# The experts' routing-weight multiply, moved from GpSimd to VectorE, in a fused two-layer attention and experts kernel

## What is computed

```python
def expert_body(y, args):
    w13_e, w2_e, c_e = args
    h = _silu_and_mul(xt @ w13_e.T)
    return (y + c_e[:, None] * (h @ w2_e.T), None)
y, _ = lax.scan(expert_body, jnp.zeros_like(xt), (w13, w2, comb.T))
y = y + _silu_and_mul(xt @ w13_s.T) @ w2_s.T
```

## Time and profile before

| | us |
|---|---|
| median of 3 runs (lowest to highest) | 1751.99 (1751.29 to 1755.93) |
| the profiled execution | 1752.64 |
| its span | 1750.8 |
| VectorE busy | 1214.8 (69% of the span) |
| TensorE busy (matmul) | 967.0 (55%) |
| ScalarE busy | 556.0 (32%) |
| GpSimd busy | 118.9 (7%) |

### The profile page before, as it was taken

The page is one execution under the profiler, slowest core; times in us unless marked ns, Lnnn a source line. Parts: engine busy times, 40 slices in busy tenths (PEclk is TensorE's granted clock), DMA queues, the critical chain, the costliest instruction groups (busy, mean ns, idle before and its releaser), DMA issues. The chain is left out here.

```text
span 1750.8 us, 29056 instructions
## 1 busy us (share of the span) xinstructions
PE 967.0 (55%) x10272; PEld 600.1 (34%) x10272; DVE 1214.8 (69%) x3031; ACT 556.0 (32%) x1210; POOL 118.9 (7%) x168
## 2 busy tenths in 40 slices
PE   4555564656455675476536556556635667354454
PEld 2443452434133252244324235234413335131112
DVE  4566763667699874476689886467779996534995
ACT  2332222535232320354433221244524321044220
POOL 0000000111001000020101000002100000020000
PEclk8575675788567786687767777678858787686586
DMA  3000000200113100110012200020022210021220
GB/s 115 1 8 8 8 2 13 50 7 1 57 49 73 31 2 7 38 26 8 5 65 70 71 1 2 13 49 8 1 57 61 69 23 2 14 48 35 83 76 7
DMA packets 48741, 55.34 MB, mean 32 GB/s; under 512 B 21200, under 2 KB 27344, under 8 KB 48400
## 3 DMA queue, kind: packets, MB, share of 16 engines
q1 hardware_dynamic: 48592, 53.42, 12.1%
HBM read 49.73 MB, written 3.67 MB: 31 GB/s over the span
## 5 line engine op out<-in xcount | busy, mean ns | idle before, releaser
L687 PE MATMUL bank<-tparts,onehot 128*128 128x64 bf16 x3840 | 164.6, 210 | 74.3 <-DVE onehot L1406 74.1
L687 PEld LDWEIGHTS bank<-tparts,onehot 128*128 128x128 bf16 x3840 | 154.6, 110 | 98.6 <-issue 55.1
L1636 DVE TENSOR_TENSOR_SCAN SG<-big 128x512 f32<-128x512 f32 x128 | 150.6, 1218 | 6.9 <-DVE GT L1422 2.1
L1406 DVE TENSOR_SCALAR onehot<-ib,CO 128x512 bf16<-128x512 f16 x320 | 106.6, 395 | 54.3 <-ACT ib L995 46.0
L995 ACT ACTIVATE ib<-bank 128x512 f16<-128x512 f32 x128 | 75.9, 596 | 180.5 <-PE bank L672 179.5
L833 PE MATMUL bank<-CV,CO 128*128 128x512 f32 x128 | 92.2, 860 | 43.3 <-DVE CV L1646 43.3
L833 PE MATMUL bank<-XP,CO 128*128 128x512 f32 x128 | 80.6, 762 | 62.3 <-DVE XP L1646 62.1
L1119 ACT ACTIVATE big<-DEL,Aneg 128x512 f32<-128x512 f32 x128 | 84.7, 717 | 63.8 <-DVE SG L1636 52.8
L960 ACT ACTIVATE relu_s<-bank,nml 128x192 f32<-128x192 f32 (+1 forms) x128 | 53.0, 426 | 162.5 <-DVE nml L1367 162.5
L1190 POOL TENSOR_TENSOR g_s<-G,trig 128x128 f32<-128x128 f32 x64 | 40.1, 626 | 934.1 <-ACT G L1008 934.1
L510 PE MATMUL bank<-CO,relu_s 128*128 128x128 f32 (+2 forms) x256 | 47.0, 346 | 68.4 <-ACT relu_s L960 68.4
(11 more groups left out here) (306 smaller groups left out, 2163.6 us busy)
## 6 DMA issues: line engine op xcount, KB each, us to landing
BC<-bc_rows SPq DMA_DIRECT2D x128, 256.0 KB, 4.4
big<-comb_rows SPq DMA_DIRECT2D x8, 1024.0 KB, 10.0
rows_bounce<-RO SPq DMA_DIRECT2D x256, 8.5 KB
W<-w SPq DMA_DIRECT2D x1, 2818.0 KB, 14.8
RB<-rows_bounce SPq DMA_DIRECT2D x16, 136.0 KB, 2.1
X<-x SPq DMA_DIRECT2D x4, 256.0 KB, 2.9
out<-CV SPq DMA_DIRECT2D x4, 256.0 KB, 2.5
big<-w SPq DMA_DIRECT2D x1, 576.0 KB, 7.5
```

Source lines behind the costliest of these rows:

```text
L687: m = mm(bank[2 + c % 2][:, (4 * (r % 2) + q) * 64:(4 * (r % 2) + q + 1) * 64], onehot[:, r % 2, kt, q * P:(q + 1) * P], tparts[:, kt, par ...
L1406: m = TS(onehot[:, r % 2, kt, :], ib[:, r % 2, :], co("pos")[:, kt:kt + 1], None, ALU.is_equal)
L1636: m = dve.tensor_tensor_scan(hs[:, j, :], dA[:, n % 2, j, :], dBu[:, n % 2, j, :], 0.0, ALU.mult, ALU.add)
```

## The change

The multiply by the routing weights is taken out of GpSimd's program and put into VectorE's, right behind the product with the up projection. The waits for `y_part` (the buffer `HT` is free) and `cb_sb` (the routing weights have landed) go with it.

```diff
             def rest(b, alone=False):
 
                 pool.wait_ge(rest_done.sem, rest_done.at(b, 0))
-                for _ in range(ROUTE_PHASES + 1):
-                    yield
-                for p in range(8):
-                    pool.wait_ge(hu_ok.sem, hu_ok.at(b, p + 1))
-                    if p >= 1 + alone:
-                        pool.wait_ge(y_part.sem, y_part.at(b, p - alone))
-                    pool.wait_ge(cb_sb.sem, cb_sb.at(b, 2))
-                    pool.tensor_tensor(HT_turn[turn_of(alone, p)], SG_turn[turn_of(alone, p)][:, 1, :], CB[:, p, :], ALU.mult).then_inc(ht_ok.sem, ht_ok.up())
-                    yield
-                    yield
-                for _ in range(EXPERT_PHASES - 17 + NORM_PHASES + SCAN_IN_PHASES + DS + SCAN_OUT_PHASES + NORM_PHASES + TOP1_PHASES):
+                for _ in range(ROUTE_PHASES + EXPERT_PHASES + NORM_PHASES + SCAN_IN_PHASES + DS + SCAN_OUT_PHASES + NORM_PHASES + TOP1_PHASES):
                     yield
...
                     TT(dst, SGp[0:rows, 1, :], bank[k0 + 1][0:rows, :], ALU.mult).then_inc(hu_ok.sem, hu_ok.up())
                     dve.wait_ge(hu_ok.sem, hu_ok.now(b))
+                    if p < 8:
+                        if p >= 1 + alone:
+                            dve.wait_ge(y_part.sem, y_part.at(b, p - alone))
+                        dve.wait_ge(cb_sb.sem, cb_sb.at(b, 2))
+                        TT(HT_turn[turn_of(alone, p)], SGp[:, 1, :], CB[:, p, :], ALU.mult).then_inc(ht_ok.sem, ht_ok.up())
                     yield
```

## The result

| | before | after |
|---|---|---|
| median (lowest to highest), 22 runs each | 1751.14 (1744.23 to 1755.96) | 1756.93 (1746.65 to 1761.86) |
| ratio, 95% interval | | 1.003 (1.0019 to 1.0042) |
| the profiled execution, its span | 1752.64, 1750.8 | 1757.68, 1755.9 |

The changed kernel comes out 0.3% slower where 0.17% faster was forecast. Two repeats, beside other runs of the kernel before, gave less: 1.0012 (0.9987 to 1.0036) and 0.9998 (0.9986 to 1.001), 12 runs each. Over all 46 runs of the changed kernel the mean is 1754.7 us, over all 171 of the kernel before 1751.0. So the loss is some 4 us, 0.2%, and one set of runs can miss it by over 0.2%.

What follows compares the result with a forecast made beforehand. No engine was full, VectorE fullest; nothing in the woven rows waited for the multiply's result, only the last stage's chain did. Woven rows -0.5 and last stage -2.4 gave -2.9 us: 1749.1 us as median, range 1743.5 to 1755.

Steps and rivals of the forecast that it cites:

- The price of the multiply: One multiply on VectorE, start to start: 0.83 us, bounds 0.69 (waits free) and 0.93; 24 in the woven rows, 19.9 us.
- p = 0: First pair, woven rows: the multiply fits into VectorE's 2.52 us idle before ScalarE's logs, 0.7 us to spare; cost 0.
- p = 1 to p = 4: Woven-row pairs: faster comparisons, no sine wait and faster copies against 0.83 us each; net 0, -0.3, -1.05, +0.36 us.
- the walk: Pair-by-pair costs in woven row 1, including +0.83 us at the sixth pair and 0 at the next two; sum -0.16 us.
- The sum of the woven rows' pairs: Three woven rows at -0.16 us each, -0.5 us: 19.9 us of new VectorE work comes out at about nothing.
- rows 2 and 3 of the program repeat its pattern: Assumption that the costs found in row 1 hold in the other two woven rows, so -0.16 us each.
- The refunds: VectorE time regained per woven row: 1.28 us in comparisons at p = 2, 1.88 for sines, 0.47 in copies.
- The rival that the refunds fail: Gather rounds wait for ScalarE's copy of `G`, so p = 2 to p = 5 cost 0.83 each: +7.6 us, 1759.6; chance 0.07.
- The port that both engines share: VectorE and GpSimd lock each other out: comparison pairs 1.6 to 1.9 us beside GpSimd's multiply, 0.62 without; sine products could collide.
- The last stage: Row 3's `rest` alone, multiply in the serial chain: -0.57 us at p = 0, -0.61 at p = 2, 4, 6; sum -2.4.
- an us is left for TensorE's clock: Last allowance in the range's upper end, beyond 1753.9 us: 1 us for the clock falling otherwise in single stretches, giving 1755.
- three signs that the prediction names of being wrong: VectorE waits for `y_part`; the pairs' stage grows over a us per row; or the last stage keeps its length.

## Why the prediction was wrong, step by step

- **The price of the multiply** was taken as 0.83 us (0.69 to 0.93) and measured 0.72 at p = 1, 3, 4 and 5 and 0.62 at p = 2 in the two rows of the loop, and 0.61 throughout in the row that is written out, where a dependent instruction starts 0.72 us after its product instead of 0.83 to 0.94. Right in kind, a little too dear.
- **p = 0** cost nothing in the woven rows, as said: the only wait of VectorE for the spread weights is the 7.3 us of the last stage.
- **p = 1 to p = 4.** The comparisons fell to 0.61 us, the 1.98 us for the sines went, the `PBD` copies lost 0.47. Where the forecast had a doubt, that later rounds may be less well fed, it was justified: up to the next subtraction p = 2 gained 0.94 us, and 0.82 of it came back in the round behind, by the new wait of 0.76 for the sines.
- **Term by term** the walk is off by more than its sum. Change of the time from one product with the up projection to the next (us, means of three profiles each):

| behind p | forecast | rows 0 and 1, each | row 2 |
|---|---|---|---|
| 0 | 0 | 0.01 | -0.09 |
| 1 | 0 | +0.26 | +0.21 |
| 2 | -0.3 | -0.21 | +0.12 |
| 3 | -1.05 | -1.48 | -1.54 |
| 4 | +0.36 | +0.51 | +1.72 |
| 5 | +0.83 | +0.58 | +0.55 |
| 6 | 0 | -1.05 | -0.67 |
| 7 | 0 | +0.58 | -0.02 |
| ahead of p = 0 and behind p = 8 | not treated | +0.48 | 0.00 |
| sum | -0.16 | -0.3 | +0.3 |

- **The sum of the woven rows' pairs** was -0.5 us and came out at -0.3, means of three profiles each. That the two agree so closely is luck: single profiles of the changed kernel lie between 322.1 and 326.9 us, p = 3, 4, 6 and 7 were mis-sized and cancelled, and "rows 2 and 3 of the program repeat its pattern" fails at p = 4 of the row that is written out. The refunds were put at 3.5 us a row (1.13, 1.88 and 0.47) and the multiplies at 3.3; the kernel with no multiply puts them at 1.6 and, against the 324.4 us with one, 1.5. The claim that 16 to 20 us of new work on the fullest engine come to about nothing in these stages stands. The rival that the refunds fail wanted 10.0 us more in these stages and falls. It would have named about the right sign for the wrong reason.
- **The port that both engines share.** The exclusive lock that the Trainium skill describes (page "SBUF — State Buffer", section "Who interferes with whom") fits the comparisons: 1.6 to 1.9 us beside GpSimd's multiply, 0.61 without it. Its other half, that the new multiply would collide with the sine products, no run here shows: not one of the 128 sine products lies in time over a multiply. That an instruction of VectorE with two inputs in SBUF is held up beside GpSimd does show, in the combining product of 1.14 us instead of 0.29.
- **The last stage** was put at -2.4 us and gave -4.9 (means), -4.5 in the first pair of profiles. The mechanism held: in the first pair, in the forecast's terms, -0.82 at p = 0 (forecast -0.57), then -0.68, -1.59 and -0.68 for three periods (-0.61 each), and -0.78 behind them (nothing). The term left out is TensorE's clock, at the full level for 27 us, in which TensorE waits 1.46 to 1.99 us for `HT` at a time instead of 2.21 to 2.66. That the shorter gaps kept the clock up is argued, not tested alone; but the last pairs took 56.0 to 56.4 us in all twelve profiles with VectorE's multiply there and 59.0 to 62.8 in all eight with GpSimd's.
- **The step that failed** is the last one of the range: "an us is left for TensorE's clock". The sum priced only the stages whose code changes and let all others keep their length. They took 9.2 us more, 7.0 of it in the norm and scan-out stages. Without that the result would have been -0.3 - 4.9 = -5.2 us, some 1747, inside the range; with it, it is +4.0. None of the three signs that the prediction names of being wrong could have told: they look at the stages whose code changes, VectorE never waits for `y_part`, the pairs stay within 1 us a row by the means, and the last stage is shorter.
- **Busy times** were forecast at about 1231 and 78 and came out at 1226.6 and 78.6.

Within the stages compared above, the clock is the cause of the length: the same matmuls take longer at the low level, and VectorE's longer waits for their results make up 3.1 of 3.1 us and 3.4 of 3.7. What stays open is why the change lets the clock be low there more often, and what the pairs have to look like for the short form. The +9.2 us rest on three profiles each, which lie from 1058.9 to 1063.0 and from 1065.8 to 1073.4 us (the changed kernel's third comes from another chip), and the scans' 1.6 us of them were not traced to a cause. They could not be switched on and off by one edit; the nearest to it is the doubled multiply, three profiles of which have the short forms in rows 0 and 1, with norm stages of 75.3 to 76.5 us.

## What to carry to other kernels

Where TensorE is little more than half busy and its clock changes level many times, an edit that moves instructions by less than a us is worth what the stages downstream make of it. Cut the profile into stages and compare those whose code is the same: what they gain or lose is the edit's too, and a forecast from the touched stages alone needs, by the spread seen here, some +-10 us in 1750 for it. Take the part of a change that pays by itself: here the last row on VectorE, which won 0.3%, and with GpSimd's multiply one phase later 0.6%. And repeat a verdict of 0.3% in another set of runs: of three for the same kernel one said 1.003 and one 0.9998.

## What was not expected of the hardware

- Lengths of the same stage recur to some 0.1 us between kernels and executions, as if there were a few forms of it: in rows 0 and 1 most are 75.0 to 75.5, 77.2 to 77.4 or 79.0 to 79.1 us for the norm, and 35.0 to 35.1, 35.9 to 36.1 or 38.0 us for the scan-out. The Trainium skill (page "TensorE: Matmul & The Clock Gate", section "Part 1: The HAM clock gate (the "warmup" mystery)") says that the same kernel sees a different number of slow matmuls from run to run and puts the penalty of the slow start at under 1% of a typical kernel. The traces agree with the first: row 0's norm stage of the kernel before was granted 0.59 of the clock in one execution and 0.67 in the other, and the stretch to the first route, the same code in all, took 297.6 to 306.7 us in twenty profiles. The second speaks of the start, and here the level changes all through the kernel; the 9.2 us are 0.5% of it and were enough to turn the sign.
- On VectorE the multiply never got slower in company. The changed kernel's view of the tile `HT` (shortest, median and longest in ns, first and last start):

```profile
L1551 DVE TENSOR_TENSOR HT<-SG,big x28: 691/691/693, 329.8 to 1579.3; 128x512 f32<-128x512 f32 x28
```

  On GpSimd the same 28 had taken 1292 ns on average.
